# A graph network of four layers on one core: softmax preparation later, layernorms placed afresh, bias and residual seeded in PSUM

## What is computed

```
x = LN(x + L0(x)); x = LN(x + L1(x)); x = LN(x + L2(x)); x = LN(x + L3(x))
L0: y = (adj @ x + x) @ W0 + b0;  y = y / max(|y|, 1e-12)
L1: 5 steps of  m = adj @ h
    z = sigmoid(m,m @ w3.T + b3 + h @ u3.T + ub3);  r = sigmoid(m,m @ w4.T + b4 + h @ u3.T + ub3)
    c = tanh(m,m @ w5.T + b5 + (r*h) @ u5.T + ub5);  h = (1-z)*h + z*c
L2: A = adj + I; d = rowsum(A)**-0.5;  y = (d*A*d) @ x @ W2.T + b2
L3: m = adj > 0; idx = cumsum(m over all cells) - 1; S = softmax(where(m, e[idx], -9e15), axis 1)
    y = diag(S)*(x @ W3[0]) + (S without diagonal) @ (x @ W3[1]) + b3
```

## Time and profile before

| | us |
|---|---|
| median of three runs | 800.88 |
| lowest, highest | 800.42, 801.36 |
| the profiled execution | 799.98 |
| its span | 798.3 |
| TensorE, DVE busy in the span | 770.0, 651.3 |
| ScalarE, POOL busy in the span | 515.2, 117.1 |

### The profile page before, as it was taken

One profiled execution on the slowest core, in us unless ns is written; L12 is line 12 of the kernel. 1 busy time (PEld: TensorE's weight loads), 2 busy tenths in 40 slices (PEclk: granted clock), 3 DMA queues, 4 the chain that ended last, 5 costly groups with the idle time before them and its releaser, 6 DMA issues.

```text
span 798.3 us, 12062 instructions
## 1 busy us (share of the span) xinstructions
PE 770.0 (96%) x3822; PEld 638.7 (80%) x3824; DVE 651.3 (82%) x1578; ACT 515.2 (65%) x1050; POOL 117.1 (15%) x127
## 2 busy tenths in 40 slices
PE   7999988899999999999999999999999999999996
PEld 6888766687888888888888888888877787888885
DVE  6788999988877777777778777777999999986444
ACT  4768756678666666666666666666677766665445
POOL 1354422200000000000000000000112133332222
PEclk9999999999999999999999999999999999999998
DMA  6300000100100000000000000000000000000112
GB/s 186 128 1 2 1 0 1 53 1 9 45 1 0 1 1 0 0 0 0 0 0 0 0 0 0 0 1 1 1 1 1 1 2 1 1 0 14 53 54 93
DMA packets 8782, 13.09 MB, mean 16 GB/s; under 512 B 2336, under 2 KB 3872, under 8 KB 8480
## 3 DMA queue, kind: packets, MB, share of 16 engines
q1 hardware_dynamic: 8736, 12.53, 4.6%
HBM read 7.28 MB, written 5.24 MB: 16 GB/s over the span
## 4 chain that ended last, share of the span: by engine, by line
PE 67%; DVE 24%; ACT 5%; issue 2%; DMA 1%; SPq 0%; POOL 0%; ACTq 0%
PE agg_ps L930 11%; PE agg_ps L932 11%; PE agg_ps L931 11%; PE gate_ps L860 5%; PE gate_ps L862 5%; PE gate_ps L861 5%; PE cand_ps L860 3%; PE cand_ps L862 3%; DVE stats L765 3%; PE cand_ps L861 3%; PE turn_ps L969 3%; PE gate_ps L867 3%; PE cand_ps L867 3%; DVE nat_lo L777 2%; DVE cand L733 2%
## 5 line engine op out<-in xcount | busy, mean ns | idle before, releaser
L576 POOL TENSOR_TENSOR rstd<-mean_var,half 128x4 f32<-128x4 f32 x64 | 78.5, 1226 | 570.6 <-DVE mean_var L772 570.5
L930 PE MATMUL agg_ps<-adj_hi,nat_hi 128*128 128x512 f32 x384 | 151.9, 396 | 0.0
L932 PE MATMUL agg_ps<-adj_hi,nat_lo 128*128 128x512 f32 x384 | 150.1, 391 | 0.0
L931 PE MATMUL agg_ps<-adj_lo,nat_hi 128*128 128x512 f32 x384 | 149.6, 390 | 0.0
L462 ACT ACTIVATE reset_hi<-gate_r 128x512 fp32r<-128x512 f32 x80 | 50.6, 632 | 105.2 <-DVE gate_r L741 105.2
L724 DVE TENSOR_TENSOR agg_lo<-agg_ps,agg_hi 128x512 fp32r<-128x512 f32 x80 | 55.1, 689 | 63.6 <-ACT agg_hi L429 63.5
L390 ACT ACTIVATE res<-res,shift,rstd 128x128 f32<-128x128 f32 x210 | 87.9, 484 | 10.1 <-DVE shift L784 10.1
L932 PEld LDWEIGHTS agg_ps<-adj_hi,nat_lo 128*128 128x128 f32 x384 | 72.0, 188 | 16.1
L931 PEld LDWEIGHTS agg_ps<-adj_lo,nat_hi 128*128 128x128 f32 x384 | 72.2, 188 | 15.6
L930 PEld LDWEIGHTS agg_ps<-adj_hi,nat_hi 128*128 128x128 f32 x384 | 72.2, 188 | 15.0
L446 ACT ACTIVATE gate_r<-gate_ps,bias 128x512 f32<-128x512 f32 x80 | 55.1, 689 | 39.4 <-PE gate_ps L862 39.4
(11 more groups left out here) (174 smaller groups left out, 1705.6 us busy)
## 6 DMA issues: line engine op xcount, KB each, us to landing
res<-in_x SPq DMA_DIRECT2D x16, 256.0 KB, 5.5
out<-res SPq DMA_DIRECT2D x16, 256.0 KB, 2.0
rows<-in_adj SPq DMA_DIRECT2D x4, 256.0 KB, 3.9
mix_rows<-feat SPq DMA_DIRECT2D x1, 1024.0 KB, 3.9
later<-mix_rows SPq DMA_DIRECT2D x1, 1024.0 KB, 4.8
gate_z<-in_L_gnn_w_w SPq DMA_DIRECT2D x3, 128.0 KB, 5.4
gate_r<-in_L_gnn_bias SPq DMA_DIRECT2D x2, 64.0 KB, 5.5
gate_z<-in_L_gnn_u_w SPq DMA_DIRECT2D x2, 64.0 KB, 4.6
```

The lines of the kernel that those rows point to most:

```text
L576: pool.tensor_tensor(rstd[:, i % RING, :], mean_var[:, i % RING, :, 1], half[:, :], ALU.pow).then_inc(rstd_made, 1)
L930: pe.matmul(ps, nat_hi[:, b, k, :], m_hi[:, k, :], start=(k == 0), stop=False)
L931: pe.matmul(ps, nat_hi[:, b, k, :], m_lo[:, k, :], start=False, stop=False)
L932: last = pe.matmul(ps, nat_lo[:, b, k, :], m_hi[:, k, :], start=False, stop=(k == T - 1))
```

## The change

1. `LAGS` has a column each for L0, the steps, L2 and L3; add, statistics, norm and split of L0 come 1 (later) and 4, 7, 7 slots (earlier). In the table the turn of a last-step result is 4 slots behind for unit 80, and two fifths of a slot more for each unit after it, up to 10.
2. Statistics no longer add epsilon or make `shift` on DVE: POOL does both, four small operations for a unit. DVE norms half the rows in L0, all of the last unit, and none elsewhere.
3. In L2 and L3 there is no bias product and no add behind the products. In slot s DVE writes `res + bias_rows` into the bank of unit s (the **seed**), the products add to it, and statistics and norm read the bank.
4. The picking of values is spread over slots 24-36 (`CHOSEN_AT`, `LATE_AT`, `VALUE_AT`), Exp stands in slots 99-102, its weighing in 104 and 105, on ScalarE; the matrix without its diagonal is selected row by row on POOL. `mix` and `chosen` lie over `eye_hi` and `eye_lo`, `count` and `mask` in `later`.
5. For L2, `adj` is loaded once more, scaled on ScalarE (slots 38, 39) and turned by TensorE with the diagonal added (slots 41-44); the eight POOL products and `d_row` are gone.
6. The loop starts one step later, with two rounds in place of three.

```diff
-LAGS = {"turn": (0, 0), "add": (1, 1), "stats": (6, 1), "shift": (7, 2), "norm": (11, 3), "split": (12, 4),
-        "back": (13, 5)}
+LAGS = {"turn": (0, 0, 0, 0), "add": (2, 1, None, None), "stats": (2, 1, 1, 1), "norm": (4, 3, 2, 2), "split": (5, 4, 3, None),
+        "cross": (5, None, 10, None), "back": (6, None, 11, None)}
...
-    return STATE_LAG if is_step(u) else 2 if stage(u) == L0 else 1
+    if is_inner(u):
+        return STATE_LAG
+    return 2 if stage(u) == L0 else STATE_LAG + (u - LAST) * 2 // 5 if is_step(u) else 1
...
+CHOSEN_AT = [B + 8 + 3 * k for k in range(T)]
+LATE_AT = [at + 2 for at in CHOSEN_AT]
+VALUE_AT = [at + 2 for at in CHOSEN_AT]
+SCALE_AT = VALUE_AT[-1] + 3
+L2_AT = SCALE_AT + 3
...
+EXP_AT = AFTER + 3
+INV_AT = EXP_AT + T
+WEIGH_AT = INV_AT + 1
+DIAGONAL_AT = INV_AT + 2
+MIX_AT = WEIGH_AT + 2
...
+        def sums(n):
+
+            return res[:, n % B, :, :] if n < AFTER else layer_ps[n % 4][:, :].rearrange("p (t d) -> p t d", t=T)
...
                 for t in range(first, end):
-                    last = act.activation(res[:, n % B, t, :], res[:, n % B, t, :], ACT.Identity,
+                    last = act.activation(res[:, n % B, t, :], summed[:, t, :], ACT.Identity,
...
                 k = s - EXP_AT
                 if 0 <= k < T:
-                    act.wait_ge(max_made, k + 1)
-                    act.activation(mix[:, k, :], mix[:, k, :], ACT.Exp, bias=row_max[:, k:k + 1],
+                    act.wait_ge(mix_loaded, 16)
+                    act.activation(later[:, k, :], later[:, k, :], ACT.Exp, bias=row_max[:, k:k + 1],
                                    accum_out=exp_sum[:, k:k + 1]).then_inc(exp_made, 1)
...
+                for k in range(2 * (s - WEIGH_AT), 2 * (s - WEIGH_AT) + 2):
+                    if 0 <= k < T:
+                        act.wait_ge(exp_inv_made, 1)
+                        act.wait_ge(diag_apart, k + 1)
+                        act.activation(later[:, k, :], later[:, k, :], ACT.Copy,
+                                       scale=exp_inv[:, k:k + 1]).then_inc(mix_made, 1)
...
                 for n in norms_at(s, "stats"):
                     i = NORMED.index(n)
-                    pool.wait_ge(stats_made, i + 1)
-                    pool.tensor_tensor(rstd[:, i % RING, :], mean_var[:, i % RING, :, 1], half[:, :],
-                                       ALU.pow).then_inc(rstd_made, 1)
-                k = s - L2_ROWS_AT
-                if 0 <= k < T:
-                    pool.wait_ge(turn_read, reads(TURN_NO["d_row", 0]))
-                    pool.tensor_tensor(later[:, k, :], later[:, k, :], d_row, ALU.mult).then_inc(l2_made, 1)
-                k = s - EYE_AT
-                if 0 <= k < T:
-                    pool.wait_ge(eye_lo_made, T)
-                    pool.tensor_tensor(later[:, k, :], eye_hi[:, k, :].bitcast(F32), eye_lo[:, k, :].bitcast(F32),
-                                       ALU.add).then_inc(eye_made, 1)
+                    pool.wait_ge(aggregated, i + 1)
+                    r = mean_var[:, i % RING, :, 1]
+                    back = shift[:, i % RING, :]
+                    link(pool.tensor_scalar(back, mean_var[:, i % RING, :, 0], -1.0, None, ALU.mult))
+                    link(pool.tensor_scalar(r, r, EPS_LN, None, ALU.add))
+                    pool.tensor_tensor(rstd[:, i % RING, :], r, half[:, :], ALU.pow).then_inc(rstd_made, 1)
+                    pool.wait_ge(rstd_made, i + 1)
+                    pool.tensor_tensor(back, back, rstd[:, i % RING, :], ALU.mult).then_inc(shift_made, 1)
...
+                if AFTER <= s < UNITS:
+
+                    wait_normed(dve, s - B)
+                    if s < AFTER + 2:
+                        dve.wait_ge(z_made, s - 2 - B + 1)
+                    elif s < AFTER + 4:
+                        dve.wait_ge(cand_made, s - 4 - B + 1)
+                    else:
+                        wait_normed(dve, s - 4)
...
+                    dve.tensor_tensor(sums(s), res[:, s % B, :, :], bias_rows[:, c:c + 1, :].to_broadcast([P, T, D]),
+                                      ALU.add).then_inc(seeded, 1)
...
+                    elif kind == "l2":
+                        pe.wait_ge(rows_scaled, T)
+                        pe.wait_ge(diag_d_made, 1)
+                        for t in range(T):
+                            cols = slice(t * P, (t + 1) * P)
+                            last = pe.transpose(to[:, cols], later[:, t, i:i + T * (P - 1) + 1:T], ident[:, :])
+                            if t == i:
+                                last = pe.matmul(to[:, cols], ident[:, :], diag_d[:, cols], start=False, stop=True,
+                                                 skip_group_check=True)
```

## The result

The changed kernel takes 777.85 us (median of four runs, 777.79 to 777.98) against 800.65 (four runs, 800.22 to 801.36) for the kernel before, run beside it: a ratio of 0.9715, interval 0.9698 to 0.9731. It is 22.8 us faster, where 20 were forecast. The profiled execution took 777.98, its span 776.2.

A forecast was written before the change was run, and what follows sets the result against it. TensorE, busy for 96%, was taken as the bound, with DVE costing excess in slots 17-31 and 87-96. Eight stretches summed to 778.5 against 798.3, 781 with overheads; forecast range 778 to 786, with rivals 773 to 790, near 0.85.

The forecast's parts named there:

- The sum: Whole kernel: stretches add to a span of 778.5 against 798.3; execution 780.2, with 0.9 for the median 781.
- Slots 0 to 16: Layernorm of L0 comes early, other engines narrowly below TensorE: 71.8 plus unchanged excess 1.2, 73.0, a gain of 1.1.
- First step: Slots 17-31: DVE freed of norms from slot 22, POOL products gone, excess about 2.5: 104.9, a gain of 17.2.
- TensorE's own work: 32 bias products (7.3) and `d_row` (0.9) gained, four L2 turns cost 2.8; slots 32-86 get 4.9 longer, 367.9.
- End of the steps: Slots 87-96: result turns stretched over slots 84-105, excess 0.6, 65.3, a gain of 6.0.
- The crossing: Slots 97-109: ScalarE overloaded, queues tied in a ring, excess 8.0 on TensorE's 54.8: 62.8, 1.1 longer than before.
- Rival A: Slots 97-109 absorb most of ScalarE's overload, excess 3.5 there, 1.5 in slots 16-19: 775.6; chance 0.22.
- B: POOL becomes the bound, 3.5 us a norm, in slots 97-109 and slots 4-15: 790; chance 0.17.
- C: A POOL power holds DVE operations with two SBUF inputs up to 1.0, in slots 7-15 and 97-109: 798; chance 0.03.
- D: Seed's ring too slow through the 31 slots of L2 and L3, losing about 46 against 20 gained: 827; chance 0.04.
- the right ring: L2 and L3: seed, product, statistics, POOL, ScalarE norm, next seed of the same bank must pass within four slots.
- POOL against DVE: Small POOL operations don't hold DVE, POOL's power is held some 0.2 to 0.4; the 128x512 product held the norm pair.

The follow-up runs named there:

- experiment 2: Kernel before, its eight 128x512 POOL products (L581, L585) cut to 128x4: 793.30 us, ratio 0.9899.
- experiment 5: Changed kernel with L0's layernorms at the old late distances, picking of values from slot 31 instead of 24, loop one step later: 780.81 us, ratio 0.9759.
- experiment 8: Changed kernel with epsilon and shift made on DVE again, shift one slot behind the statistics: 801.02 us, ratio 1.0008.
- experiment 3: Changed kernel with all 16 last-step results turned 4 slots behind their unit, in place of 4 to 10: 777.72 us, ratio 0.9713.
- experiment 6: Changed kernel with DVE norming half the rows of the results of units 90 to 94: 777.97 us, ratio 0.9723.
- experiment 10: Changed kernel with Exp in slots 98 to 101 instead of 99 to 102: 777.67 us, ratio 0.9714.
- experiment 1: Changed kernel with L0's layernorms at the old distances (statistics 8, norm 13, split 14 slots behind) and RING 16: 797.86 us, ratio 0.9954.
- experiment 11: Changed kernel with Exp from slot 98, DVE norming three of four parts for units 90 to 95, results stretched by a fifth: 779.00 us, ratio 0.9723.
- experiment 9: Changed kernel with the product of the diagonal one slot later, slot 106 instead of 105: 777.80 us, ratio 0.9715.
- experiment 7: Changed kernel with all four Exp in slot 82, in place of one each in slots 99 to 102: 780.82 us, ratio 0.9747.

## Why the prediction was right, and where it was not

**The sum.** 778.5 was given for the span, 776.2 measured. Then 0.9 was added for the distance of one profiled run from the median; after the change the two are 0.1 apart. That 0.9 was a third of the whole miss.

**Slots 0 to 16.** Term 73.0, measured 71.98. The failed step is "I leave the excess at 1.2". The slots from 8 to 12 are 4.32 or 4.33, TensorE's own price; DVE, ScalarE and POOL stayed below it as summed.

**First step.** Gain 17.2, measured 19.1. TensorE's work was right and the excess 0.6, not 2.5. The size was nearly right, the weights of its grounds were not: I put DVE's load by L0's layernorms first and the POOL products behind it. The runs divide it otherwise. The POOL products were 7.75 (experiment 2); late layernorms 3.9 to 6, of which slots 0 to 16 pay back 3.3 for taking them (experiment 5); epsilon and shift 2.9, by experiment 8 on the changed kernel. These were measured on different kernels and need not add up. What is left of 19.1, 2.5 to 4.6, was not taken apart; candidates are the weighing (four of 0.68 on DVE, 2.7) and the product of `d_row` (0.9). And with the old lags the new place of the picking would have cost 16 us by the two turn banks, which the prediction didn't see, and which the change avoids.

**TensorE's own work.** Slots 32 to 86 are 367.84 for 367.9, and L3 slots 4.99 with a turn and 4.52 without, for 4.98 and 4.51. A bias product is 0.226 where TensorE is the bound. In the crossing most of it was hidden, which the sum had in it, since it took ScalarE as the bound there.

**End of the steps.** Slots 87 to 96: 65.3 given, 66.44 measured, excess 1.7 for 0.6. The failed step is that the gain of 6.0 was put down to the stretching. It gives 2.9 there and takes 3.25 in the crossing (experiment 3). The other 2.0 are DVE's two small operations. Most of the excess that is left stands in slot 94: it has no turn and takes 7.51, with DVE busy for 7.27; it is the third slot in a row with statistics. The prediction had such slots paid back by the next free one, and as a sign that no L1 slot near the end goes above 6.7; slots 91 (6.90) and 94 went above it.

**The crossing.** Excess 8.0 given, 7.5 measured (62.32 less 54.8), 62.8 against 62.32. That ScalarE bounds it was shown: two parts of a norm less are 0.77 less (experiment 6), Exp one slot earlier is worth 1.26 (experiment 10). It is not ScalarE alone: in slot 105 it has 5.85 of 6.79, and TensorE waits 2.5 there for `diag_m` and then runs at half clock. No term of the sum stood for that, so that the total is nearer than its ground. Rival A was right that slots 97 and 98 have room; the changed kernel doesn't use it.

**The rivals.** B: POOL did not bound L0. C: the pairs of norms never took longer than 0.60. Timeline of slots 5 and 12 of the changed kernel:

```profile
37.86 1.04 POOL L600 TENSOR_TENSOR rstd<-mean_var,half 128x4 f32<-128x4 f32 x1
...
37.90 0.59 DVE L733 TENSOR_SCALAR res<-res,mean_var,rstd 128x128 f32<-128x128 f32 x2
...
64.00 1.04 POOL L600 TENSOR_TENSOR rstd<-mean_var,half 128x4 f32<-128x4 f32 x1
...
64.62 0.66 DVE L791 TENSOR_TENSOR nat_lo<-res,nat_hi 128x512 fp32r<-128x512 f32 x1
```

The power had begun 0.04 before the pair and held nothing. Rival C spoke of operations with two SBUF inputs, and they were not held either: the split beside the second power took 0.66, and all 32 seeds took 0.69 to 0.71. D did not come, but experiment 8 shows that it is real and near: at 6.3 us a slot in the crossing, close to the 6 on which I priced it. But it stays within the crossing, 19 us in 13 slots, where I had it run through all 31 slots of L2 and L3 for 46. What keeps it away is where shift is made. I gave it 0.04 and named the right ring, but not the edit of the change that prevents it.

## What to carry to other kernels

- A small instruction is priced by whose queue it stands in and who waits for it, not by its length: epsilon (0.17 us) and shift (0.15 us) on DVE cost 19 us in the crossing; on POOL, in four small instructions, they stayed off the path. Ask of each tiny step which chain closes through it.
- Moving work pays only until the next engine is full. ScalarE led DVE by 0.6 us a slot in the crossing: two parts a norm to DVE gained 1.3, three parts, with a flatter table, lost 1.
- With two banks for turns, a third turn in a slot waits for a reader at the end of the slot. Count the users of each ring of buffers per slot before work is put there.

## What the runs showed of the chip

**POOL against DVE.** A 128x512 product on POOL held a norm pair (two `tensor_scalar`, SBUF to SBUF) by 0.8 to 1.05 in 8 of 8 cases, a 128x4 product in none of 8. Small POOL operations seem to be held themselves: the first of a layernorm's four (L598) took 0.58 at 133.32 in experiment 1, beside a DVE split, where the mean of 64 in the changed kernel is 0.34 and the shortest 0.24.

The Trainium skill, "SBUF — State Buffer", section "Who interferes with whom", says that a `tensor_scalar` within SBUF can take the port pair that it shares with GpSimd, and that whoever comes first has it for the whole instruction. For the 128x512 product the trace agrees (0.60 becomes 1.65); for the power of 1.04 on 128x4 it doesn't, since the pair that began 0.04 behind it took 0.59. The prediction gave the product as agreeing with the same section's sentence on two SBUF inputs; the norm pair that it held reads one wide input from SBUF, so it bears on the sentence on `tensor_scalar`.

**The granted clock.** Between slot 1 and the end it fell to half, 1.2 GHz, now and then: from 662 to 665 us in the changed kernel, from 663 to 669 in experiment 11, from 671 to 681 in experiment 8. In the places looked at each fall came near the end of a wait of TensorE or within 1.5 us behind it: 2.0 us, ended at 129.5 and at 157.8, in the kernel before, 2.5 before 662 us in the changed one, 4.27 in slot 24 of experiment 1. But not each such wait brings one: 1.99 before 148.4 us in the kernel before, 2.98 in slot 26 of experiment 1 and 2.5 in experiment 9 left the clock at full. Where the clock fell under a TensorE that was not the bound, in slot 22 of the kernel before, the slot took 9.43 as the one behind it took 9.44; where TensorE had to catch up, as in experiments 1 and 7, I take it as paid in full, which no run isolates. What decides whether a wait brings a fall stays open.
